# A gated state-space layer with a mixture of experts: TensorE's order within a state, and the first expert weights in two loads

## What is computed

```python
xz = h @ Win; x_ssm, z = split(xz)             # 256 inner channels each
x_ssm = silu(conv1d_4(x_ssm) + conv_b)
dt = softplus(x_ssm @ dt_w + dt_b); Bt = x_ssm @ Bp; Ct = x_ssm @ Cp
state = state * exp(dt * A) + (dt * x) * B_t   # per channel, 64 states, over 512 tokens
y = sum over the 64 states of state * C_t
s = x + ((y + x_ssm * D) * silu(z)) @ Wout
h_e = gelu(rmsnorm(u) @ W1[e] + b1[e]); o_e = h_e @ W2[e] + b2[e]   # hidden size 512
ffn = u + sum of 2 shared o_e + sum of the 2 best of 8 routed o_e * gate
```

## Time and profile before

| | |
|---|---|
| median of 3 runs | 2161.35 us (2155.5 to 2163.98) |
| the profiled execution | 2163.6 us, its span 2161.9 us |
| granted TensorE clock, mean | 0.956 of full speed |
| busy, PE / weight loads / DVE / ACT / POOL | 85% / 36% / 84% / 67% / 69% |
| groups | 64: 1 first, 7 heads, 56 others |
| DVE idle behind line 1059 over the main stage | 235.2 us |

### The profile page before, as it was taken

One profiled execution on the slowest core, in us unless ns is written; L12 is line 12 of the kernel. 1 busy time (PEld: TensorE's weight loads), 2 busy tenths in 40 slices (PEclk: granted clock), 3 DMA queues, 4 the chain that ended last, 5 costly groups with the idle time before them and its releaser, 6 DMA issues.

```text
span 2161.9 us, 43970 instructions
## 1 busy us (share of the span) xinstructions
PE 1836.0 (85%) x12024; PEld 785.5 (36%) x12024; DVE 1806.3 (84%) x1972; ACT 1448.5 (67%) x2452; POOL 1488.9 (69%) x670
## 2 busy tenths in 40 slices
PE   1776788889888898888898988988888988889887
PEld 1533333333333333333333333333333333333333
DVE  7898588888888888888888788888888888888886
ACT  1577776676766767767767667667667676676672
POOL 7200277786777777777877678777777677777775
PEclk9977799999999999999999999999999999999998
DMA  5233644454444544464445444463445434555442
GB/s 143 87 131 134 182 93 112 105 126 115 99 108 118 135 110 100 100 151 110 101 109 131 118 102 100 107 144 106 112 106 133 110 104 104 129 126 108 101 102 76
DMA packets 181261, 247.86 MB, mean 115 GB/s; under 512 B 17314, under 2 KB 77164, under 8 KB 181036
## 3 DMA queue, kind: packets, MB, share of 16 engines
q1 hardware_dynamic: 181204, 247.02, 46.4%
HBM read 221.22 MB, written 25.30 MB: 114 GB/s over the span
## 4 chain that ended last, share of the span: by engine, by line
PE 48%; issue 17%; DVE 14%; ACT 12%; POOL 3%; DVEq 2%; ACTq 1%; SPq 1%; DMA 0%; POOLq 0%
PE ps L1073 15%; PE ps L1059 9%; DVE arena L903 9%; PE ps L1109 9%; PE ps L1117 7%; POOL arena L516 3%; ACT L693 3%; PE ps L1045 3%; ACT arena L677 2%; ACT arena L693 2%; PE ps L975 2%; DVE ps L893 2%; ACT arena L671 1%; SPq L255 1%; PE ps L1081 1%
## 5 line engine op out<-in xcount | busy, mean ns | idle before, releaser
L516 POOL TENSOR_TENSOR arena<-arena 128x1024 f32<-128x1024 f32 x512 | 1208.8, 2366 | 598.2 <-DVE arena L903 456.8
L903 DVE TENSOR_TENSOR_SCAN arena<-arena,ps 128x512 f32<-128x512 f32 x1024 | 1197.1, 1207 | 262.2 <-PE ps L1059 243.6
L671 ACT ACTIVATE arena<-arena,neg_A 128x512 f32 (+1 forms) x1024 | 687.2, 714 | 269.0 <-DVE arena L903 263.8
L1059 PE MATMUL ps<-arena 128*64 128x128 f32 x6144 | 439.0, 287 | 90.6 <-DVE arena L903 89.9
L1073 PE MATMUL ps<-arena,ident 64*64 64x512 f32 x3584 | 510.1, 641 | 2.1 <-POOL arena L516 2.1
L1059 PEld LDWEIGHTS ps<-arena 128*64 128x64 f32 x6144 | 344.5, 142 | 406.2 <-issue 302.5
L1109 PE MATMUL ps<-x_rms,arena 128*128 (+1 forms) x640 | 338.0, 627 | 128.0 <-ACT arena L693 122.9
L893 DVE TENSOR_TENSOR ps<-arena,ps 128x512 f32<-128x512 f32 x640 | 405.7, 680 | 1.8 <-PE ps L1045 1.8
L693 ACT ACTIVATE arena<-ps,b1r_sb 128x512 f32<-128x512 f32 x256 | 169.0, 686 | 253.8 <-PE ps L1109 253.0
L1117 PE MATMUL ps<-arena 128*128 128x512 f32 x512 | 281.6, 632 | 0.0
L677 ACT ACTIVATE arena<-ident,b_turned 128x128 f32<-128x128 f32 x768 | 242.6, 387 | 0.0
(11 more groups left out here) (128 smaller groups left out, 835.4 us busy)
## 6 DMA issues: line engine op xcount, KB each, us to landing
arena<-c_scratch SPq DMA_DIRECT2D x128, 1024.0 KB, 8.5
arena<-w_routed_scaled SPq DMA_DIRECT2D x64, 256.0 KB, 2.7
arena<-in_L_ffn_W_r_dram SPq DMA_DIRECT2D x64, 256.0 KB, 7.1
arena<-gate_scratch SPq DMA_DIRECT2D x64, 256.0 KB, 3.3
arena<-w_shared_tiles SPq DMA_DIRECT2D x128, 64.0 KB, 2.2
arena<-dt_scratch SPq DMA_DIRECT2D x9, 512.0 KB, 9.5
arena<-u_scratch SPq DMA_DIRECT2D x9, 512.0 KB, 10.4
sz_scratch<-arena SPq DMA_DIRECT2D x8, 512.0 KB, 4.2
```

What stands on the lines that cost most here:

```text
L516: nc.gpsimd.tensor_tensor(products[:, i % RING, :, :], states[:, i % 2, :, :], c_rows[:, i // CG, i % CG, :].unsqueeze(1).broadcast_to((P, ...
L671: nc.scalar.activation(decay[:, 2 * i + h, :], dflat[:, ds(slot + h * L, L)], ACT.Exp, scale=aflat[:, ds(col, 1)]).then_inc(s["decay_ready ...
L903: vector.tensor_tensor_scan(states[:, i % 2, h, :], decay[:, m, :], ps[bank][:], 0.0, ALU.mult, ALU.add).then_inc(s["scanned"], 1)
L1059: ins = mm(bank[HP * r:HP * r + HP, c * P:(c + 1) * P], u_turned[:, odd, c, h * P + HP * r:h * P + HP * r + HP], b_diag[:, e, c, :], start ...
```

## The change

PE's order within a state becomes: bcast or fill half 0 for state i + 1, `ysum`, fill half 1 for i + 1, W1 tiles, then the closing work, W2 tiles and the rest. Hidden tiles 2 and 3 move from states 0 and 1 to state 1, tile 4 from 1 to 2; tile 0 of the next group from 6 to 5 (it stays in 6 in group 7, where it waits for both copies of u). The W2 tiles 0 to 3 are made in states 4 and 5, two each. W1 comes in two loads with semaphores of their own: columns of tiles 0 and 1 (128 KB) once tiles 0 and 1 of the group before are made, the rest (128 KB, and the shared tile's 64 KB) once all five are. ACT's copies of u move one state earlier. The same instructions are issued otherwise, but for one more load per group.

```diff
@@ load_w1 @@
-                if not isinstance(b, int) or not isinstance(g, int):
+                first = isinstance(b, int) and isinstance(g, int)
+                if not first:
+                    sp.wait_ge(s["hidden_made"], b * (E * (HT + 1)) + (g * (HT + 1) - (HT - 1)))
+                sp.dma_start(w1_in[:, 0:2, :].rearrange("p n k -> p (n k)"),
+                             w1r_d[ds(g, 1), :, 0:2 * P].rearrange("e c h -> (e c) h")).then_inc(s["w1_loaded"], 16)
+                if not first:
                     sp.wait_ge(s["hidden_made"], b * (E * (HT + 1)) + g * (HT + 1))
-                sp.dma_start(w1_in[:, 0:HT, :].rearrange("p n k -> p (n k)"),
-                             w1r_d[ds(g, 1)].rearrange("e c h -> (e c) h")).then_inc(s["w1_loaded"], 16)
+                sp.dma_start(w1_in[:, 2:HT, :].rearrange("p n k -> p (n k)"),
+                             w1r_d[ds(g, 1), :, 2 * P:].rearrange("e c h -> (e c) h")).then_inc(s["w1b_loaded"], 16)
                 sp.dma_start(w1_in[:, HT, :], w1sh_d[ds(g, 1)].rearrange("e c h -> (e c) h")
-                             ).then_inc(s["w1_loaded"], 16)
+                             ).then_inc(s["w1b_loaded"], 16)
@@ ScalarE, group @@
-                    if head and not first and i in (4, 6):
-                        copy_u(b, slot, i // 2 - 2)
+                    if head and not first and i in (3, 5):
+                        copy_u(b, slot, i // 2 - 1)
@@ TensorE, tables and hidden_tile @@
-            W1_AT = {0: (2,), 1: (3, 4)}
-            W1_NEXT_AT = {6: (0,), 7: (1,)}
-            W2_AT = {2: (0,), 3: (1,), 4: (2,), 5: (3,), 7: (4,)}
+            W1_AT = {1: (2, 3,), 2: (4,)}
+            W1_NEXT_AT, W1_NEXT_BLOCK_AT = {5: (0,), 7: (1,)}, {6: (0,), 7: (1,)}
+            W2_AT = {4: (0, 1,), 5: (2, 3,), 7: (4,)}
...
-                    pe.wait_ge(s["w1_loaded"], u * 32 + 32)
+                    pe.wait_ge(s["w1_loaded"], u * 16 + 16)
+                if t == 2:
+                    pe.wait_ge(s["w1b_loaded"], u * 32 + 32)
@@ TensorE, group, in the loop over i @@
-                    for t in W1_AT.get(i, ()):
-                        hidden_tile(u, t, t0)
-                    if next_t0 is not None:
-                        if i == 6 and next_odd != odd:
-                            pe.wait_ge(s["ut_copied"], b * 2 + 4)
-                        for t in W1_NEXT_AT.get(i, ()):
-                            hidden_tile(u + 1, t, next_t0)
                     if not head or i >= LAG or last is not None:
...
                             ysum(n0, i - LAG)
+                    if ahead and KIND[ahead[1]] == "E":
+                        fill(*ahead, ahead_odd, 1)
+                    for t in W1_AT.get(i, ()):
+                        hidden_tile(u, t, t0)
+                    if next_t0 is not None:
+                        at = W1_NEXT_BLOCK_AT if next_odd != odd else W1_NEXT_AT
+                        if next_odd != odd and 0 in at.get(i, ()):
+                            pe.wait_ge(s["ut_copied"], b * 2 + 4)
+                        for t in at.get(i, ()):
+                            hidden_tile(u + 1, t, next_t0)
...
                         add_to_y(RING)
-                    if ahead and KIND[ahead[1]] == "E":
-                        fill(*ahead, ahead_odd, 1)
```

More of the change, by code:

```diff
@@ L206, in mamba_gated_moe @@
             "b_broadcast u_b_multiplied scanned decay_ready product_ready y_summed dt_u_loaded end_loaded "
-            "w1_loaded w2_loaded w2s_loaded gate_row_loaded w2_used hidden_made gelu_ready expert_made "
+            "w1_loaded w1b_loaded w2_loaded w2s_loaded gate_row_loaded w2_used hidden_made gelu_ready expert_made "
             "expert_gated expert_added decay_slot_claimed product_claimed xn_loaded y_complete y_gated "
```

## The result

| | before | changed kernel |
|---|---|---|
| median of the runs | 2160.61 us (2155.5 to 2163.98, 4 runs) | 1963.12 us (1960.85 to 1969.71, 4 runs) |
| ratio | | 0.9093, 95% interval 0.9064 to 0.9122 |
| profiled execution (span) | 2163.6 us | 1960.85 us (1959.1) |
| mean granted clock, whole span | | 0.975 |

The forecast was 1970 us, in a range from 1942 to 2030. In the changed kernel the lines are 6 to 8 higher: 909 is the scan, 1065 the fill, 1079 the sum, 1117 the hidden tile, 1125 and 1131 the W2 tiles, 1051 the broadcast, 522 POOL's product, 528 its pair sum, 918 the gate.

What follows compares the result with a forecast made beforehand. The prediction took DVE's 235.2 us of waits behind PE's fill as the bound. 30 x 2.7 + 26 x (29.68 - 25.4), less 3.5, plus 5, gave 193.8 us off 2163.6: 1970 us, range 1942 to 2030.

Steps and rivals of the forecast that it cites:

- Step 1: State 1: with its fill of half 1 ahead of hidden tile 2, DVE's 2.90 us stall goes, 28.10 to 25.20 us.
- Step 2: PE from state 6 on needs 9.76 us against DVE's 9.61: late by 0.15, taken as 0.2, period 25.4 us.
- The rival that PE is not late: PE's lateness from state 6 on would be zero, giving 1959 us; chance 0.08.
- Step 3: Hidden tile 2 moves to T = 4.8, after gelu 0 is over at 3.0; its wait disappears, cost nothing.
- The third rival: A nearly full PE meets another late input and 1.5 us a group come back: 2054 us; chance 0.12.
- Step 4: State 4's 0.28 us stall goes but counts nothing, since state 6 waits for POOL's product 4; 16 us if POOL gave way.
- Step 5: PE's half-clock stretch disappears with the two-microsecond wait, so the 26 long groups of 29.68 us fall to 25.4.
- Step 6: W2 tiles moved to states 4 and 5: W2's load starts no later, effect nothing.
- Step 7: W1 in two loads: first issued at T = 2.3, landed by 13.5 to 14, wanted at 14.5; effect nothing.
- The fourth rival: W1's first part lands late for tile 0 in state 5 and the kernel is slower, at least 2258 us at T = 21; chance 0.03.
- Step 8: Seven head groups: more PE work and later closing fills lose 0.5 us each, 3.5 us in all.
- Step 9: First group: its 6.00 us stall falls in part, POOL's first product and ACT hold DVE next; 5 us gained.

Runs made afterwards that it cites:

- experiment 1: Kernel before with only the order changed: fill of half 1 right behind the sum, ahead of the W1 tiles, tables as before; 2087.97 us, ratio 0.9647.
- experiment 3: Kernel before with one table line changed: W1 tiles 2 and 3 in state 1, tile 4 in state 2; 1982.36 us, ratio 0.9147.
- experiment 2: Changed kernel with the fill of half 1 back at the end of the state, tables kept as changed; 1949.43 us, ratio 0.9008.
- Experiment 5: Changed kernel with W2 tile 4 in state 5 instead of 7 outside head groups; 1962.17 us, ratio 0.9059.
- Experiments 8 to 10: Changed kernel, POOL's pair sum behind product 4: 1957.76 us; plus fill half 1 last, W2 tile 4 in state 5: 1929.34; plus POOL's expert addition behind product 7: 1913.81.
- Experiments 6 and 7: Kernel before with eight zero-adding matmuls ahead of hidden tile 2 outside heads: one-row stationary 2166.07 us, 120-row stationary 2124.65 us.
- Experiment 4: Changed kernel with both W1 loads behind the wait for all five hidden tiles of the group before; 1966.81 us, ratio 0.9083.

## Why the prediction was right

The time came 7 us under the forecast (1963.12 against 1970), and the working holds step by step in the profile. The cause I gave for it held only in part.

- **Step 1, the stall goes: right in size, wrong in what does it.** The 2.90 us are gone. I credited the fill's place ahead of hidden tile 2. That order alone gives half of it (experiment 1, 26.7 us a group). The table alone, which takes tile 2 out of state 0, gives nearly all (experiment 3, 25.8) or all (experiment 2, 25.25). The prediction read the two parts as one, because either of them puts the gelu's wait behind the fill.
- **Step 2, PE late: right, a little too large.** From the first scan of state 6 to the fourth of the next group the forecast had 9.76 us for PE, and it is 941.28 - 931.52 = 9.76. The lateness was forecast as 0.15 and taken as 0.2; the period is 0.18 over the 25.2, but only 0.11 of it is PE's and 0.06 POOL's last product, which the forecast didn't have. Experiment 5 shows that without PE's part 0.10 of the period goes. The rival that PE is not late is thereby excluded: 25.4, not 25.2. The Trainium skill (Perfetto Trace Analysis, Identifying the Most-Contended Engine) judges TensorE's headroom by the share of the weight loads and by that of the FLOPs, which the prediction left out; the first of the two is 41% of the main stage here, and PE's order still cost time. This trace bears out the starts of the matmuls, not that share.
- **Step 3, the moved waits: right.** Tile 2 starts at T = 942.50 - 937.76 = 4.74, forecast 4.8, without a wait. The third rival, a wait that moves, didn't come.
- **Step 4, POOL: right.** The 0.28 us in state 4 are gone and DVE's wait in state 6 grew from 0.22 to 0.60, so nothing was gained. A wait of over 0.5 us a group behind POOL stood among the signs that the forecast is wrong, and by its letter that sign came. It was set too low: step 4's own terms, 0.22 and 0.28, already make 0.50, and the time was counted with them. Experiments 8 to 10 show it from the other side: with POOL's pair sum out of the way the group falls to 24.8.
- **Step 5, the clock: right in the ordinary groups.** The main stage has 1.00, and no ordinary group is long for the clock; the third head has a stretch at half clock, which costs 0.90 us (its wait for the residual is 2.89 instead of 1.99). I named 0.98 as the mean to be seen; the whole span has 0.975, because stage one counts in it, which I had not set apart. Experiments 6 and 7 show that this term is about 41 us of the gain, near the 26 x 1.58 that the prediction's rows give. The Trainium skill (TensorE: Matmul & The Clock Gate, What's actually happening) has activity as what releases the throttle; the second of those runs agrees; in the first, PE was as busy in the profile and the stretch stayed.
- **Step 6, W2's tiles: nothing lost, and something gained.** Experiment 3, which leaves them in states 2 to 5, has a wait of 1.10 us in state 4 that experiment 2 hasn't. The prediction priced this part at nothing; with what else differs between the two kernels it is worth 0.6 us a group.
- **Step 7, W1 in two loads: right in ordinary groups.** The load went out at T = 3.4, not 2.3, landed in 4.0 us (the median over both loads), and tile 0 asked for it at T = 15.4. Experiment 4 shows that the split does nothing. In heads PE does wait for it, 4.1 us in all seven. The fourth rival, the late landing that makes the kernel slower, thus had its beginning where it was said to be thinkable, and no more.
- **Step 8, heads: right in sum by luck.** -3.9 us against -3.5. The plain heads lost 0.6 to 0.7 us each where 0.5 was forecast, and the steps within them came as walked. But the head that was walked is the third, one of the two that are longer than the plain ones before too (35.5 against 35.0), and these two lost 3.8 us together, which was not forecast; the half-clock stretch of head 4, which went, gave 2.5 back. A plain head, of DVE:

```profile
1090.02 2.33 DVE L909 TENSOR_TENSOR_SCAN arena<-arena,ps 128x512 f32<-128x512 f32 x2
...
1101.87 1.29 DVE L863 TENSOR_TENSOR arena<-ps,arena 128x512 f32<-128x512 f32 x2 [2.56 <-PE ps L1087]
...
1109.92 0.69 DVE L871 TENSOR_TENSOR arena<-ps,arena 128x512 f32<-128x512 f32 x1 [1.99 <-PE ps L1096]
...
1121.05 0.69 DVE L881 TENSOR_TENSOR arena<-ps,arena 128x512 f32<-128x512 f32 x1 [0.76 <-PE ps L1102]
```

The closing product comes at T = 11.85 (forecast 12.1), the residual at 19.9 (20.2), and the result is 0.76 late (0.75). On heads 3 and 5 see below.

- **Step 9, the first group: too high.** 3.1 us instead of 5. The wait of 6.00 us is gone whole, and 3.19 us come back behind POOL's product; I had named POOL but not priced it. A wait of 1.96 us for the fill's first half stands in both kernels.

Against the profiled execution (1960.85) the forecast was 9 us too high: the main stage saved 195.6 us instead of 193.8, and 7.2 lie outside it, 5.9 of them in stage one.

## What to carry to other kernels

When one engine's queue is in a fixed order, look for the instruction with the latest input ahead of what the critical engine wants, and price both ways of removing it: moving the wanted one forward, or moving the late one back. Here the second gives 94% of the gain in one line of a table, and the first gives 39% and costs time when both are done, for the most part because it pulls half fills ahead of what closes a head (11.5 of the 17 us are in the heads). Then take the next wait in the list: here two instructions of POOL, moved by a few products, and W2's last tile gave another 1.8% (1949.43 to 1913.81 us) once the forward move was undone. Each time look at the rare groups too: what shortens 56 groups can lengthen the other seven.

## What was not expected

- **Filling a wait is not enough for the clock.** Eight matmuls with one row of zeros as stationary took 1.90 us in PE's timeline, and 28 of 56 ordinary groups stayed long for the half clock; with the selection matrix of 120 rows, as long, none did.
- **An operation of DVE that took three times as long beside POOL.** Line 876 reads and writes the arena alone, and waits for no product of POOL. In 21 heads of experiments 8 to 10 POOL was in an instruction when it started; it took 1.97 to 1.99 us and ended some 0.54 us after that instruction. In the seven heads of the changed kernel and of the kernel before POOL started 0.16 us behind it, and it took 0.67. In experiment 2 it started behind POOL in five heads, later in POOL's instruction, took 1.23 to 1.25, and again ended some 0.54 us after it. The scans, which also read PSUM, take 1.22 us at most in the changed kernel, whether POOL is in an instruction or not.
- **PE after a jump of the loop.** The loop over pairs of blocks jumps back ahead of heads 3 and 5, which are 37.8 and 37.0 us long. In the first of them PE's first half fill comes 2.56 us after the first scan (877.37 - 874.81), in the plain head 1091.36 - 1090.02 = 1.34. In the kernel before it came 2.46 late in that same head (957.95 - 955.49) and was in the main hidden by the stall for the gelu, since the head is 35.5 long and the plain ones 35.0. Of the 2.1 us by which head 3 is longer than a plain one in the changed kernel 1.2 are this, 0.9 the half-clock stretch. In experiment 1 such a head shows it plainly, with nothing that PE waits for:

```profile
924.61 1.09 PE L1059 MATMUL ps<-arena 128*64 128x128 f32 x16 [2.77 <-issue]
925.63 1.94 PE L1073 MATMUL ps<-arena,ident 64*64 64x512 f32 x8
```

These two heads are the longest of the seven in seven of the ten other kernels as well (41.1 and 36.5 in the fastest, where the others are 34.0 to 34.4). That the jump is the cause is read from where they stand; no run took the jump away, so it stays open.
- **The gain of a better order can be smaller in total than in its groups.** Experiments 5 and 8 shortened the ordinary groups (by 0.10 and 0.5 us on the mean) and lost nearly all and 71% of it in seven heads.
